# Stack loads one half step earlier, and the late norms and low weight parts on GpSimd, in a gated two-layer transformer kernel

## The reference

```
x = x + tanh(g_xattn[0]) * L0_xattn(layernorm(x), ctx)     # 8 heads, softmax over 256, per batch
x = x + tanh(g_ffn[0])   * L0_ffn(layernorm(x))            # 8 experts (256 -> 512 -> 256), top-p weights
x = x + tanh(g_xattn[1]) * L1_xattn(layernorm(x), ctx, mask)   # scores, masked softmax, readout of ctx
x = x + tanh(g_ffn[1])   * L1_ffn(layernorm(x))            # 4 experts (64 tokens of each), 256 -> 256 -> 256
```

```
def _L1_ffn_ref(x, gate_up_proj, down_proj):
    x4 = x.reshape(B, G, E, H)
    gu = jnp.einsum('bgeh,ehd->bged', x4, gate_up_proj)
    gate, up = (gu[..., :I], gu[..., I:])
    inter = jax.nn.silu(gate) * up
    out = jnp.einsum('bgei,eih->bgeh', inter, down_proj)
```

## Time and profile before

| | before |
|---|---|
| median of 3 runs | 874.48 us (869.98 to 880.75) |
| the profiled execution | 879.49 us, its span 877.8 us |
| mean granted clock of TensorE | 0.957 of full speed |
| PE / PEld busy | 780.0 us (89%) / 724.0 us (82%) |
| DVE / ACT / POOL busy | 687.1 (78%) / 596.3 (68%) / 580.6 us (66%) |
| queue of SyncE and ScalarE (q1) | 72.2% of the 16 DMA engines' span |

### The profile page before, as it was taken

One profiled execution on the slowest core, in us unless ns is written; L12 is line 12 of the kernel. 1 busy time (PEld: TensorE's weight loads), 2 busy tenths in 40 slices (PEclk: granted clock), 3 DMA queues, 4 the chain that ended last, 5 costly groups with the idle time before them and its releaser, 6 DMA issues. The chain is left out here.

```text
span 877.8 us, 30099 instructions
## 1 busy us (share of the span) xinstructions
PE 780.0 (89%) x11511; PEld 724.0 (82%) x11511; DVE 687.1 (78%) x2385; ACT 596.3 (68%) x1298; POOL 580.6 (66%) x617
## 2 busy tenths in 40 slices
PE   3464689999999999999999989999999899888976
PEld 2343478999999998999999989999999898777875
DVE  3674778888787888888887868787888686798973
ACT  3365768878787877787787868787878673454442
POOL 4264646778778787879788868888878573222321
PEclk9855679999999999999999999999999999999999
DMA  6569999788878888789898978879798765110002
GB/s 229 164 139 207 244 199 227 139 151 140 163 141 151 154 146 153 145 151 148 154 154 153 157 129 143 159 152 150 139 157 135 129 109 146 49 50 26 25 2 97
DMA packets 319541, 122.99 MB, mean 140 GB/s; under 512 B 274717, under 2 KB 312613, under 8 KB 319397
## 3 DMA queue, kind: packets, MB, share of 16 engines
q1 hardware_dynamic: 318656, 120.53, 72.2%
q10 hardware_dynamic: 740, 0.54, 0.2%
HBM read 45.53 MB, written 8.39 MB: 61 GB/s over the span
## 5 line engine op out<-in xcount | busy, mean ns | idle before, releaser
L591 POOL TENSOR_TENSOR p_parts<-p,p_parts 128x512 f16<-128x512 f32 x256 | 296.6, 1159 | 134.0 <-ACT p_parts L706 118.3
L846 PE MATMUL psG<-xT,w_gu 128*128 128x128 f16 x3072 | 195.3, 221 | 6.6 <-DVE th_ga_h L1282 6.1
L583 POOL TENSOR_TENSOR hp_lo<-th_ga_h,hp_hi 128x512 f16<-128x512 f32 x136 | 157.6, 1159 | 57.9 <-ACT hp_hi L728 54.6
L846 PE MATMUL psU<-xT,w_gu 128*128 128x128 f16 x3072 | 192.5, 219 | 1.4 <-DVE th_ga_h L1290 1.3
L846 PEld LDWEIGHTS psG<-xT,w_gu 128*128 128x128 f16 x3072 | 178.2, 99 | 11.0 <-DVE th_ga_h L1282 9.0
L846 PE MATMUL psY<-w_dn,hp_hi 128*128 128x256 f16 x1024 | 182.5, 274 | 0.5 <-POOL hp_lo L583 0.5
L846 PEld LDWEIGHTS psU<-xT,w_gu 128*128 128x128 f16 x3072 | 175.8, 98 | 3.2 <-DVE th_ga_h L1290 2.6
L706 ACT ACTIVATE p_parts<-p 128x512 f16<-128x512 f32 x256 | 160.5, 627 | 6.9 <-DMA p_turn<-p_parts 6.2
L1206 DVE CUSTOM_DVE_ANT_0 ps<-ps,mask_in 128x256 f32<-128x256 f32 x256 | 104.2, 448 | 70.0 <-PE ps L846 69.4
L698 ACT ACTIVATE p<-ps,exp_bias 128x256 f32<-128x256 f32 x256 | 106.9, 469 | 64.9 <-DVE exp_bias L1210 63.9
L846 PE MATMUL psY<-w_dn,hp_lo 128*128 128x256 f16 x512 | 140.1, 274 | 0.0
(11 more groups left out here) (180 smaller groups left out, 1052.9 us busy)
## 6 DMA issues: line engine op xcount, KB each, us to landing
mask_in<-in_mask_Bx2048x_ff SPq DMA_DIRECT2D x32, 256.0 KB, 3.5
part_scratch<-parts SPq DMA_DIRECT2D x16, 384.0 KB, 4.1
q_stack<-part_scratch SPq DMA_DIRECT2D x62, 96.0 KB
k_stack<-part_scratch SPq DMA_DIRECT2D x62, 96.0 KB
stage<-in_L_ffn_gate_w SPq DMA_DIRECT2D x8, 512.0 KB, 5.1
stage<-in_L_ffn_up_w SPq DMA_DIRECT2D x8, 512.0 KB, 4.7
stage<-in_L_ffn_down_w SPq DMA_DIRECT2D x8, 512.0 KB, 4.4
p_turn<-p_parts SPq DMA_TRANSPOSE x256, 3.6
```

Source lines behind the costliest of these rows:

```text
L583: pool.tensor_tensor(hp_lo[:, u % 2, :], hb32[:, u % 2, :], hp_hi[:, u % 2, :], ALU.subtract).then_inc(s["h_split"], 1)
L591: pool.tensor_tensor(p_parts[:, g % 4, 1, :, :], p32[:, g % 2, :, :], p_parts[:, g % 4, 0, :, :], ALU.subtract).then_inc(s["plo_done"], 1)
L846: return pe.matmul(out_, lhsT, rhs, start=start, stop=stop, skip_group_check=shares_bank)
```

## The change

Three things. SyncE's stack pieces go out at half steps 5, 7, 9 and 11 of a pair instead of 6, 8, 10 and 12, and the mask's load at half step 0 of a step instead of 1. The late norms go from VectorE to GpSimd, right behind the power that they need. The low parts of the late weights go from VectorE's fused operations to GpSimd: for each of an expert's two pieces a scaling in place and a subtraction; the small piece follows one half step after the large one.

```diff
@@ SyncE
-                    if i == 1 and 1 <= n and n + 1 < B:
+                    if i == 0 and 1 <= n and n + 1 < B:
                         sp.wait_ge(s["max_done"], 16 * n)
                         load_mask(n + 1, (n + 1) % 2)
...
-                    if even and i == 6 and q + 1 < NPAIR:
+                    if even and i in (5, 7) and q + 1 < NPAIR:
                         sp.wait_ge(s["scores_done"], 8 * n)
-                        load_stacks(sp, 1 - par, q + 1, 0)
-                    if not even and i in (0, 2, 4) and q + 1 < NPAIR:
-                        load_stacks(sp, 1 - par, q + 1, 1 + i // 2)
+                        load_stacks(sp, 1 - par, q + 1, i // 2 - 2)
+                    if not even and i in (1, 3) and q + 1 < NPAIR:
+                        load_stacks(sp, 1 - par, q + 1, 2 + i // 2)
@@ GpSimd
-            def late_pow(t, kind):
+            def late_norm(t, kind):
                 pool.wait_ge(s[f"ln{3 + kind}_in"], t + 1)
-                pool.tensor_tensor(crs[:, kind, :], cve[:, kind, :], minus_half[:, 0:2], ALU.pow
-                                   ).then_inc(s[f"pow{3 + kind}_done"], 1)
+                st.link(pool.tensor_tensor(crs[:, kind, :], cve[:, kind, :], minus_half[:, 0:2], ALU.pow))
+                if t:
+                    pool.wait_ge(s[f"xn{3 + kind}T"], t)
+                for u in range(2):
+                    pool.tensor_scalar((xn3, xn4)[kind][:, u, :], x_res[:, 2 * t + u, :], cmv[:, kind, u, 0:1],
+                                       crs[:, kind, u:u + 1], ALU.subtract, ALU.mult).then_inc(s[f"xn{3 + kind}_ready"], 1)
+            def late_w_low(e, piece):
+                (src, dst), (_, high) = late_weight(e, 1)[piece], late_weight(e, 0)[piece]
+                pool.wait_ge(s["dw_hi"], 4 * e + 2 * piece + 2)
+                st.link(pool.tensor_scalar(src, src, W_SCALE, None, ALU.mult))
+                pool.tensor_tensor(dst, src, high, ALU.subtract).then_inc(s["dw_split"], 2)
...
                         if r == 4:
-                            late_pow(t, 1)
+                            late_norm(t, 1)
                         if r == -2:
-                            late_pow(t, 0)
+                            late_norm(t, 0)
+                    for piece in range(2):
+                        e = late_cut_at(n, i - piece) if i >= piece else late_cut_at(n - 1, i + 8 - piece)
+                        if e is not None:
+                            late_w_low(e, piece)
@@ VectorE: late_w_low and late_norm are gone, and their calls
-                        elif r == -1:
-                            late_norm(t, 0)
-                        elif r == 5:
-                            late_norm(t, 1)
-                    if e is not None:
-                        late_w_low(e)
```

More of the change, by code:

```diff
@@ L146, in build @@
             c_exp pT_ready pT_done read_done xn4T xn4_hi xn4_split cx0_loaded cx1_loaded
-            d_yevac d_yT d_out xn3_ready xn4_ready xn3T cxT ln3_in ln4_in pow3_done pow4_done out0_stored out1_stored
+            d_yevac d_yT d_out xn3_ready xn4_ready xn3T cxT ln3_in ln4_in out0_stored out1_stored
             mask_m_loaded bd_ready""".split()
@@ L1325, in _ @@
             norm1_stats(2, STATS_AHEAD)
-            def late_w_low(e):
-                dve.wait_ge(s["dw_hi"], 4 * e + 4)
-                for (src, dst), (_, high) in zip(late_weight(e, 1), late_weight(e, 0)):
-                    dve.scalar_tensor_tensor(out=dst, in0=src, scalar=W_SCALE, in1=high,
-                                             op0=ALU.mult, op1=ALU.subtract).then_inc(s["dw_split"], 2)
             def late_stats(t, kind):
@@ L1342, in late_stats @@
                 dve.tensor_scalar(cve[:, kind, :], cmv[:, kind, :, 1], EPS, None, ALU.add).then_inc(s[f"ln{3 + kind}_in"], 1)
-            def late_norm(t, kind):
-                dve.wait_ge(s[f"pow{3 + kind}_done"], t + 1)
-                if t:
-                    dve.wait_ge(s[f"xn{3 + kind}T"], t)
-                for u in range(2):
-                    dve.tensor_scalar((xn3, xn4)[kind][:, u, :], x_res[:, 2 * t + u, :], cmv[:, kind, u, 0:1],
-                                      crs[:, kind, u:u + 1], ALU.subtract, ALU.mult).then_inc(s[f"xn{3 + kind}_ready"], 1)
             def late_masks(t):
```

## The result

The changed kernel takes **885.98 us** (four runs, 883.38 to 887.05) beside 873.25 us of the kernel before, measured next to it: a ratio of 1.0114, with a 95% interval of 1.0083 to 1.0145. It is slower by 1.1%, where 857.8 us and 1.9% faster were forecast. The profiled execution took 885.63 us, its span is 883.7 us, the mean granted clock 0.948.

A forecast was written before the change was run, and what follows sets the result against it. TensorE was taken to bound the middle, VectorE's order the late rounds. Gains of 15.5 and 3.65, 19.2 us, gave 860.3 from the profiled execution or 855.3 from the median; the middle, 857.8 us, was forecast, 8-in-10 range 850 to 872.

The forecast's parts named there:

- The bound in the middle: Middle of the run: TensorE is the bound, 99.68 us busy of the 100 from 400 on, at full clock.
- Stack loads: SyncE's pieces issued about 2.0 us earlier would remove TensorE's waits for the stacks and the clock drops: 15.5 us gained.
- 11.6 + 2.9 = 14.5: Stack waits after the early one: 11.6 us of twelve waits go, and two clock drops with them, 2.9 us.
- Of the early 2.55 us I count 1.0: First stack wait, at 86.66: 1.0 us gained, between 0 and 2.55, since p_turn is late there too.
- (a): Stack loads: full DMA engines, not issue order, hold the last piece; the 15.5 us stay, about 873; chance 0.13.
- (c): Stack loads: the store of parts lands late, slower than before from 7.2 us on; about 895 at 8.5; chance 0.04.
- Late half: Last layer: norms and low parts moved to GpSimd shorten rounds from 14.2 to 13.2 us; 3.65 us gained, between -2 and 8.
- What hides GpSimd's time is its idleness: Late rounds: idle time covers GpSimd's added work, except at hp_lo, for which TensorE would wait 1.4 to 1.9 us.
- the first norm: Start of the late part: this operation on GpSimd delays hp_lo, which TensorE takes at once: 0.9 us lost.
- 1.0 + 0.55: Late part: 1.0 us gained in two rounds without low parts, 0.55 as the last norm no longer runs beside hp_lo.
- VectorE as the pace: Past 740 us VectorE's order sets the rounds: busy 12.89 of 14.2 us, TensorE 12.05 and the floor once VectorE is relieved.
- Rival (b): Late rounds: VectorE and GpSimd lock each other out, VectorE's small product stretched; rounds of 14.6 us, 864 in all; chance 0.18.

The follow-up runs named there:

- e1: Kernel before with only the SyncE part of the change (new places of stack and mask loads); late work stays on VectorE: 858.6 us.
- e2: Changed kernel with SyncE's part undone: norms and low parts on GpSimd, loads at their old half steps: 900.95 us.
- e15: e1 with the first pair's stack pieces back at half steps 6, 8, 10 and 12: 865.7 us.
- e11: Changed kernel with late norms (after the first pair) and scalings on GpSimd covering half their columns, near forecast prices; the rest left out: 865.5 us.
- e6: Changed kernel with GpSimd scaling the weights by a two-input multiplication with a constant column: 881.2 us.
- e16: e14 with VectorE's late norms also cut to one column each after the first pair: 847.7 us.
- e3: Changed kernel with the low parts of the weights back on VectorE; norms stay on GpSimd, new loads: 873.0 us.
- e10: e1 plus, behind each power on GpSimd, a norm pair's work into a spare tile nobody reads: 872.6 us.
- e12: e3 with GpSimd's norms issued a half step later, behind hp_lo: 881.4 us.
- e8: e4 with ScalarE scaling the weights, so that GpSimd only subtracts: 861.8 us.
- e13: e8 with both subtractions of an expert in the same half step: 860.2 us.
- e9: e1 with the late norms on ScalarE as scale and shift, the shift made by GpSimd; low parts on VectorE: 867.4 us.
- e17: e9 with VectorE's low parts of the first three experts made three half steps later: 858.6 us.
- e18: e1 with VectorE's low parts moved three half steps later, as in e17; norms on VectorE: 860.0 us.
- e4: Changed kernel with the norms back on VectorE; low parts of the weights stay on GpSimd, new loads: 868.8 us.
- e14: e1 with the second layer's low parts left out, GpSimd writing zeros in their place: 858.3 us.

## Why the prediction was wrong

**The bound in the middle: right.** TensorE is busy 100.00 us of the 100 from 400 on, after 99.68.

**Stack loads: mechanism right, one term too small.** All but one of the thirteen waits for the stacks are gone, in the changed kernel as in e1. Each is left with one of 0.4 us; e1's line is

```profile
PE ps L846 <- DMA k_stack<-part_scratch: 0.4, 1, 0.4
```

From the third store of parts (issued at 193.91 before, 188.64 in e1) to the first late power it is 550.8 us before and 535.6 in e1, 15.2 less, where 11.6 + 2.9 = 14.5 were forecast. The size holds over all traces: 550.8 and 551.8 with the old loads (before, e2), 533.7 to 537.7 with the new. Ahead of that store lie 5.3 us, where 1.0 was: "Of the early 2.55 us I count 1.0" took the wait at 86.66 for all there was to gain, while e15 puts 7.1 us on the first pair's loads. By medians, though, the whole is 16.6 and not 20.5, near the 15.5 forecast; which part of the traces' gain the shorter executions of the kernel before lack, no trace shows. That e1's 858.6 lies near the 857.8 forecast for both halves is luck: a late gain of 3.65 was in the forecast, and e1 has none. The store of the parts lands after 3.2 us at least, 3.9 in the median and 6.6 at most, where it was 3.1, 4.1 and 6.1; rivals (a) and (c) did not come.

**Late half: the step that failed is GpSimd's price.** The prediction put the single-input operations "nearer the cast"; they measured 2.44 us a pair instead of 0.9 to 1.4, and 1.50 and 2.78 instead of 0.75 and 1.35. With the subtractions that is 4.9 + 7.6 = 12.4 us more a cut round, instead of 2.3 + 5.4 = 7.7. GpSimd then has 16.2 us, more than the 14.2 of the round. The prediction held that "What hides GpSimd's time is its idleness"; it priced delays behind single operations and never made this sum for GpSimd's whole round, although its range for the late half was open only to 2 us of loss. At nearly the forecast prices (e11) 22.0 of the 26.0 us do not occur; that is shown. The Trainium skill's line in "GPSIMD Engine Reference", section "Engine selection", by which one-input work is near line rate on GpSimd, does not hold for these forms: at 1024 columns the scaling took 2.78 us, the two-input subtraction 2.13, and the same scaling in two-input form 1.89 (e6).

**What the price set off.** TensorE's waits grew by 15.2 us, and the clock cost 10.9 more. The prediction knew of such drops (1.46 us after a wait of 2.25) and counted them only where they went away, not where its own new waits would bring them.

**Terms that were off at any price.** In e11 the two middle rounds are 13.65 us, near the 13.2 forecast. But the round ahead of the cut ones is 13.3 instead of 10.8 (0.9 was allowed for the first norm), and the last cut round is 17.1, with 3.7 us at the late gate, where the round was to come out even; in the changed kernel that wait is 6.05. These two (1.6 and 2.9 us over what was allowed) are 4.5 of the 7.7 us between e11 and the forecast. Behind the cut rounds e11 lost 1.0 us on e1, where 1.0 + 0.55 were to be gained; that is 2.6 more, and its cause stays open.

**VectorE as the pace: right, but not for sale at that price.** Without both kinds of work the rounds are 11.8 us (e16), 12.2 us of late part better than before. Each engine that took work over gave the gain back, in whole or nearly: GpSimd by making in turn what had been made side by side (e3, e10, e12) and by locking VectorE out (e8, e13), ScalarE, in e9, by the place of its cast. How much of the ceiling is VectorE's time and how much the place of its work (e17, e18) is open.

**Rival (b)** named the lock-out and its place, and both are there: the small product took 2.04 us in two rounds of e4 and 0.88 in e13, 0.16 when alone. It is not what made the changed kernel slow. There the small product took 0.16, 0.16, 0.16 and 0.70 us in the four cut rounds, and TensorE's waits for VectorE in the late part fell from 15.1 us before to 1.7. In e4 it has a larger share: VectorE's remaining work took 8.9 us longer than the same work in e1 (105.6 instead of 104.3 - 7.6), 3.8 of them the small product. How much of the weights' 7.7 us that makes was not separated, as e14, the kernel without subtractions, has a lock-out of its own.

The chance of "faster", 0.43, is 0.04 above what the prediction counts up for it (half of 0.52, and 0.13).

## What to carry to other kernels

Before work is moved to an idle engine, add up that engine's whole round at prices of the very operation form; where the trace lacks the form, let the range reach well past the dearest of the near rows (here a norm took 1.22 us, beside a two-input row of 0.70 and a cast of 0.45), and ask whether the engine is still idle then. Ask also what the engine makes at that same moment: two results that two engines made side by side become one late result on one engine, in either order. And a new wait on a TensorE that runs at full clock is to be priced with the clock's fall behind it; here that was two fifths of the loss.

## What the hardware showed

GpSimd's one-input operation with a scalar was dearer than its two-input operation of the same size: 2783 against 2129 ns at 1024 columns, 1502 against 1153 at 512 (float32 in; the former writes float32 in place, the latter 16 bits). The type written is not the reason: as a two-input operation, with the constant in a column that is repeated, the same scaling in place took 1894 and 1038 ns (e6). With two column scalars, 256 columns took 1224 ns and 128 columns 797. Next to that a cast of 256 columns had taken 449.

VectorE's operation of 128x2 elements took 1.56 us beside a GpSimd subtraction instead of 0.21. It started at 769.27 and ended at 770.83, the subtraction at 768.67 and 770.80; so the lock lasts by the other's instruction, whatever one's own size. The Trainium skill, "SBUF — State Buffer", section "Who interferes with whom", says that the engine which issues first has the shared ports for the whole instruction; the rows of e4, e8 and e13 agree. In e14 operations on GpSimd that only write did it too: a norm pair that began at 766.89, beside its zeros from 767.08 to 768.49, took 2.06 us instead of 0.73.
